# Cross attention in a decoder kernel: query scale and maximum moved into the exponential, its row sums accumulated there, the mask product cut to the x keys

## The reference, cut to what matters

```python
q = rms_norm((x @ wq).reshape(B, L, 16, 128), q_norm_w)
k = rms_norm((x @ wk).reshape(B, L, 4, 128), k_norm_w)
k_ctx = rms_norm((h_ctx_kv @ wk_ctx).reshape(B, T, 4, 128), k_norm_w)
q = q * cos + rotate_half(q) * sin
k = k * cos + rotate_half(k) * sin
k_full = concatenate([k_ctx, k], axis=1)   # 64 context keys, 64 x keys
v_full = concatenate([v_ctx, v], axis=1)
mask = concatenate([zeros((L, T)), causal], axis=1)
scores = einsum('blhd,bmhd->bhlm', q, k_full) / sqrt(128) + mask
probs = softmax(scores, axis=-1)
out = einsum('bhlm,bmhd->blhd', probs, v_full).reshape(B, L, 2048) @ wo
```

## Time and profile before

| | |
|---|---|
| median of 3 runs | 2205.65 us (2205.2 to 2206.36) |
| time of the profiled execution | 2202.77 us |
| its span | 2200.9 us |
| PE busy | 1804.3 us, 82% |
| DVE busy | 1608.8 us, 73% |
| ACT busy | 1061.2 us, 48% |
| POOL busy | 789.9 us, 36% |
| mean granted clock of TensorE | 0.947 |

### The profile page before, as it was taken

How to read it: one execution, slowest core, us unless ns; L and a number is a source line. 1 busy time by engine, 2 the same in 40 slices (tenths; PEclk the granted TensorE clock), 3 DMA queues, 4 the chain that set the end, 5 groups by cost and what they waited for, 6 DMA issues and landing times. The chain is left out here.

```text
span 2200.9 us, 42393 instructions
## 1 busy us (share of the span) xinstructions
PE 1804.3 (82%) x14872; PEld 1064.3 (48%) x14944; DVE 1608.8 (73%) x2887; ACT 1061.2 (48%) x2086; POOL 789.9 (36%) x924
## 2 busy tenths in 40 slices
PE   5999999778889899868874773777777199999998
PEld 2666666446666666654443441222222155555555
DVE  6555555489989989956995996999996447575744
ACT  2444444345555555533332771888888033333322
POOL 5754321366666665547773333112211000000000
PEclk9999999889999999989987995999999599999999
DMA  8511000100000000001110111122221000000000
GB/s 229 140 40 35 21 2 0 44 20 8 11 12 11 7 7 6 1 20 58 57 40 21 42 37 27 44 57 55 59 56 35 24 1 1 10 0 10 0 10 10
DMA packets 71351, 69.74 MB, mean 32 GB/s; under 512 B 14224, under 2 KB 60048, under 8 KB 71184
## 3 DMA queue, kind: packets, MB, share of 16 engines
q1 hardware_dynamic: 70416, 65.46, 10.5%
q0 software_dynamic: 768, 2.10, 0.3%
HBM read 54.16 MB, written 9.96 MB: 29 GB/s over the span
## 5 line engine op out<-in xcount | busy, mean ns | idle before, releaser
L205 PE MATMUL ps<-arena 128*128 128x512 f16 (+6 forms) x6424 | 1106.4, 326 | 76.5 <-POOL arena L1025 20.7
L205 PEld LDWEIGHTS ps<-arena 128*128 128x128 f16 (+1 forms) x6464 | 608.4, 100 | 476.9 <-issue 76.1
L1430 DVE TENSOR_REDUCE arena<-ps 128x4 f32<-128x1024 f32 x256 | 304.7, 1218 | 21.9 <-PE ps L1343 21.9
L1413 ACT ACTIVATE arena<-ps 128x512 f32<-128x512 f32 x512 | 278.5, 598 | 83.8 <-PE ps L1351 60.8
L2121 DVE TENSOR_TENSOR arena<-ps,arena 128x512 f32<-128x512 f32 x96 | 66.4, 691 | 174.4 <-ACT arena L1984 142.2
L1343 PE MATMUL ps<-arena 31*128 31x256 f16 x1024 | 103.3, 278 | 90.2 <-ACT arena L1413 53.6
L1979 ACT ACTIVATE arena<-arena 128x512 f16<-128x512 f32 x96 | 60.4, 629 | 230.3 <-DVE arena L2131 230.2
L1398 PE MATMUL ps<-arena 128*32 128x256 f32 x2048 | 164.0, 392 | 2.6 <-ACT arena L1420 0.6
L534 POOL TENSOR_TENSOR arena<-arena 64x256 f32<-64x256 f32 x128 | 77.9, 609 | 206.8 <-DVE arena L473 195.9
L925 POOL TENSOR_TENSOR arena<-arena 128x512 f32<-128x512 f32 x80 | 107.7, 1346 | 97.6 <-DVE arena L851 97.2
L930 POOL TENSOR_TENSOR arena<-arena 128x512 f32<-128x512 f32 x96 | 105.8, 1102 | 94.0 <-DVE arena L847 87.7
(11 more groups left out here) (205 smaller groups left out, 3114.3 us busy)
## 6 DMA issues: line engine op xcount, KB each, us to landing
arena<-in_L_ffn_gate_up_proj SPq DMA_DIRECT2D x12, 512.0 KB, 3.6
ch_out<-arena SPq DMA_DIRECT2D x32, 128.0 KB
arena<-in_L_ffn_down_proj SPq DMA_DIRECT2D x6, 512.0 KB, 3.6
ch_keys<-arena SPq DMA_DIRECT2D x48, 64.0 KB, 2.0
arena<-ch_keys SPq DMA_DIRECT2D x64, 48.0 KB
arena<-arena SPq DMA_DIRECT2D x192, 16.0 KB
arena<-in_x SPq DMA_DIRECT2D x4, 512.0 KB
arena<-in_L_attn_wq_codes SPq DMA_DIRECT2D x8, 256.0 KB
```

The lines of the kernel that those rows point to most:

```text
L205: last = nc.tensor.matmul(out, a, b, start=start and n == 0, stop=stop and n == len(pairs) - 1, skip_group_check=not group)
L1413: nc.scalar.activation(pT[:, b % 3, g], ps[:, T[n % len(T)], :].rearrange("p (u t) -> p u t", u=KD), ACT.Exp, scale=CH_SCALE).then_inc(s_e ...
L1430: nc.vector.tensor_reduce(m[:, half % 2, 2 * half_pair:2 * half_pair + 2, j, :], ps[:, bank(user):bank(user) + 2, :].rearrange("p g (u s) ...
```

## The change

The queries are rotated and turned without their norm. The norm's factor of each token and head, times 1/sqrt(128), is laid out in a small tile `qscale` by four POOL instructions for each 128 tokens. VectorE still takes the maximum of the raw scores, then multiplies it by `qscale` and -1 into `negtop` (128 x 4) and no longer subtracts. ScalarE computes the exponential straight from PSUM, in four instructions of 128 x 128 in place of one of 128 x 512, each with `qscale` as its scale, `negtop` as its bias and a column of `total` as its accumulator output. The row-sum instruction of VectorE goes. POOL multiplies only the two key turns of a tile by the norm; the flips of the queries wait for the sum (`joined`) in place of the product (`scaled`). The mask product covers the 64 x keys of each of the four blocks, 256 columns in place of 512. The next scores wait for the exponential (`exped`) and no longer for the subtraction (`shifted`), as both read bank SC.

```diff
-                        pe.wait_ge(shifted.sem, shifted.at(i, k))
-                        nc.tensor.matmul(ps[:, SC, :], ident[:, :], mask[:, :, :].rearrange("p a b -> p (a b)"), start=True, stop=False, skip_group_check=True)
+                        pe.wait_ge(exped.sem, exped.at(i, k))
+                        nc.tensor.matmul(ps[:, SC, :].rearrange("p (c m) -> p c m", c=4)[:, :, S:CROSS_KEYS], ident[:, :], mask[:, :, :], start=True, stop=False, skip_group_check=True)
...
-                            pe.wait_ge(scaled.sem, scaled.at(i, n + 1))
+                            if u < 2:
+                                pe.wait_ge(scaled.sem, scaled.at(i, 2 * s + u + 1))
+                            else:
+                                pe.wait_ge(joined.sem, joined.at(i, n + 1))
...
-                        act.wait_ge(shifted.sem, shifted.at(i, k + 1))
+                        act.wait_ge(negated.sem, negated.at(i, k + 1))
                         act.wait_ge(probs.sem, probs.at(i, k - 1))
-                        nc.scalar.activation(e[:, k % 2], shift[:, k % 2], ACT.Exp, scale=CROSS_SCALE).then_inc(exped.sem, 1)
+                        for c in range(4):
+                            last = nc.scalar.activation(e[:, k % 2, c, :], ps[:, SC, c * CROSS_KEYS:(c + 1) * CROSS_KEYS], ACT.Exp,
+                                                        bias=negtop[:, k % 2, c:c + 1], scale=qscale[:, s % 2, g].rearrange("p b r -> p (b r)")[:, c:c + 1],
+                                                        accum_out=total[:, k % 2, c:c + 1])
+                        last.then_inc(exped.sem, 1)
...
-                        dve.wait_ge(probs.sem, probs.at(i, k - 1))
-                        nc.vector.tensor_tensor(shift[:, k % 2], sc, spread(top[:, k % 2, :], CROSS_KEYS), ALU.subtract).then_inc(shifted.sem, 1)
+                        dve.wait_ge(scales_set.sem, scales_set.at(i, 4 * (s + 1)))
+                        nc.vector.scalar_tensor_tensor(out=negtop[:, k % 2, :], in0=top[:, k % 2, :], scalar=-1.0, in1=qscale[:, s % 2, g].rearrange("p b r -> p (b r)"),
+                                                       op0=ALU.mult, op1=ALU.mult).then_inc(negated.sem, 1)
...
-                        nc.vector.tensor_reduce(total[:, k % 2, :], e[:, k % 2], AX.X, ALU.add).then_inc(totalled.sem, 1)
-                        dve.wait_ge(totalled.sem, totalled.at(i, k + 1))
                         nc.vector.reciprocal(inv[:, k % 2, :], total[:, k % 2, :]).then_inc(inverse.sem, 1)
...
-                            a4 = a.rearrange("p (r d) -> p r d", d=CROSS_HD)
-                            nc.gpsimd.tensor_tensor(a4, a4, spread(rms[:, s % 2, u * CROSS_KVH:(u + 1) * CROSS_KVH], CROSS_HD), ALU.mult).then_inc(scaled.sem, 1)
+                            if u < 2:
+                                a4 = a.rearrange("p (r d) -> p r d", d=CROSS_HD)
+                                nc.gpsimd.tensor_tensor(a4, a4, spread(rms[:, s % 2, u * CROSS_KVH:(u + 1) * CROSS_KVH], CROSS_HD), ALU.mult).then_inc(scaled.sem, 1)
+                        if g == 0:
+
+                            pool.wait_ge(exped.sem, exped.at(i, CROSS_KVH * (s - 1)))
+                            heads = rms[:, s % 2, 2 * CROSS_KVH:CROSS_NORMS].rearrange("p (g r h) -> p g r h", r=2, h=2)
+                            pool.wait_ge(scaled.sem, scaled.at(i, 2 * (s + 1)))
+                            for b in range(2):
+                                for r in range(2):
+                                    nc.gpsimd.tensor_scalar(qscale[r * S:(r + 1) * S, s % 2, :, b, :], heads[b * S:(b + 1) * S, :, :, r], CROSS_SCALE, None,
+                                                            ALU.mult).then_inc(scales_set.sem, 1)
+                                    pool.wait_ge(scales_set.sem, scales_set.at(i, 4 * s + 2 * b + r + 1))
```

More of the change, by code:

```diff
@@ L598, in cross_stage @@
     joined = tally("joined", SUBS * CROSS_TURNS)
-    scaled = tally("scaled", SUBS * CROSS_TURNS)
+    scaled = tally("scaled", SUBS * 2)
+    scales_set = tally("scales_set", SUBS * 4)
     turned, turn_kept = tally("turned", SUBS * CROSS_TURNS), tally("turn_kept", SUBS * CROSS_TURNS)
     scored = tally("scored", CROSS_UNITS)
-    maxed, shifted, totalled, inverse = (tally(c, CROSS_UNITS) for c in ("maxed", "shifted", "totalled", "inverse"))
+    maxed, negated, inverse = (tally(c, CROSS_UNITS) for c in ("maxed", "negated", "inverse"))
     exped = tally("exped", CROSS_UNITS)
@@ L629, in cross_stage @@
         qT = sb("qT", [P, 2, 2, CROSS_REP * S], F32)
-        top, total, inv = (sb(c, [P, 2, 4], F32) for c in ("top", "total", "inv"))
-        shift, prob = (sb(c, [P, 2, 4, CROSS_KEYS], F32) for c in ("shift", "prob"))
-        e = shift
+        top, negtop, total, inv = (sb(c, [P, 2, 4], F32) for c in ("top", "negtop", "total", "inv"))
+        qscale = sb("qscale", [P, 2, CROSS_KVH, 2, 2], F32)
+        e, prob = (sb(c, [P, 2, 4, CROSS_KEYS], F32) for c in ("e", "prob"))
         pT = sb("pT", [P, 2, 2, CROSS_REP * S], F32)
@@ L636, in cross_stage @@
         table = sb("table", [P, 2, 2, CROSS_HD], F32)
-        mask = sb("mask", [P, 4, CROSS_KEYS], BF16)
-        maskf = sb("maskf", [P, CROSS_KEYS], F32)
+        mask = sb("mask", [P, 4, S], BF16)
+        maskf = sb("maskf", [P, S], F32)
         ident = sb("ident", [P, P], BF16)
@@ L813, in _ @@
             settle(core, dve, "x")
-            credit(dve, xn, x_lo, summed, rooted, roped, maxed, shifted, totalled, inverse, o_lo, added)
+            credit(dve, xn, x_lo, summed, rooted, roped, maxed, negated, inverse, o_lo, added)
             half = CROSS_HD // 2
@@ L824, in make_tables @@
                 nc.vector.tensor_copy(ident[:, :], core.ident[:, :])
-                nc.vector.tensor_copy(mask[:, :, :], maskf[:, :].unsqueeze(1).broadcast_to([P, 4, CROSS_KEYS]))
+                nc.vector.tensor_copy(mask[:, :, :], maskf[:, :].unsqueeze(1).broadcast_to([P, 4, S]))
                 dve.drain().then_inc(s_tables, 1)
@@ L877, in body @@
                             dve.wait_ge(summed.sem, summed.at(i, CROSS_TURNS * (s + 1)))
-                            dve.wait_ge(scaled.sem, scaled.at(i, CROSS_TURNS * (s - 1)))
+                            dve.wait_ge(scaled.sem, scaled.at(i, 2 * (s - 1)))
+                            dve.wait_ge(scales_set.sem, scales_set.at(i, 4 * (s - 1)))
                             rsqrt(core, dve, rooted, i, RSQRT_STEPS * s, sums[:, s % 2, :], CROSS_RMS_EPS, rms[:, s % 2, :], root)
@@ L904, in _ @@
         def _(pool):
-            credit(pool, c_hi, c_lo, joined, scaled, probs)
+            credit(pool, c_hi, c_lo, joined, scaled, scales_set, probs)
             ctx = core.ins["ctxT"].rearrange("(k p) n -> p k n", p=P)
@@ L2181, in constants @@
     future = key[None, :] > query[:, None]
-    mask = np.concatenate([np.zeros((P, S)), np.where(future, -1e9, 0.0)], 1)
+    mask = np.where(future, -1e30, 0.0)
     start = 2.0 ** (-2.0 ** (-(np.log2(ALIBI_HEADS) - 3)))
```

1 line of the change is left out of this document (added).

## The result

| | before | after |
|---|---|---|
| median of 4 runs | 2206.01 us (2205.20 to 2207.89) | 2232.02 us (2231.38 to 2233.71) |
| profiled execution, its span | 2202.77, 2200.9 us | 2233.71, 2231.9 us |
| mean granted clock | 0.947 | 0.937 |
| the stage, first normalisation row (line 170) of it to that of the next stage | 423.45 to 981.74, 558.3 us | 422.74 to 1004.41, 581.7 us |

The changed kernel is slower: ratio 1.0118 (95% interval 1.0100 to 1.0135), 26 us, where 5 were forecast. The predicted range ended at 2226. In the profiles the stage itself is 23.4 us longer; what follows it took 1219.2 us before and 1227.5 after. In this study's other kernels, whose code there is the same, it took 1217 to 1228, so these 8 us are no more than it varies by without a change there.

A forecast was written before the change was run, and what follows sets the result against it. The prediction took the chain from VectorE's maximum through ScalarE to PE's second flip as the bound. Waits +14.2, mask -5.9 and start -3.2 gave +5.1 us: 2207.9 us profiled, 2211 us median, range 2189 to 2226.

The forecast's parts named there:

- The bound: In the steady stage, one chain from VectorE's maximum through ScalarE to PE's second flip, 36.3 us of waits.
- VectorE's relief: VectorE loses 1.1 us a step, so its lateness at the maximum, 18.2 us in all, is gone.
- The exponentials: On ScalarE, four of 0.36 + 0.20 us each: 2.24 us until the next copy, in place of 0.54.
- Rival 1: Row sums on ScalarE free or nearly so: four exponentials take 1.44 us, total 2188 us; chance 0.32.
- rival 2: Exponentials don't overlap, each accumulator being written out first: 2.72 us, total 2225 us; chance 0.16.
- The product: VectorE's new four-column instruction behind the maximum, priced like the reciprocal: 0.18 us and 0.04 to its reader.
- D: Change in length of the chain from maximum to second flip: forecast +1.20 us; the total changes sign at 1.02.
- 29 D - 29.7: The forecast's total change in us as a function of the chain's lengthening; +5.1 us as forecast.
- The start: Before 495 us, fewer POOL query products give VectorE about 3.1 us, shortening two second-flip waits: -3.2 us.
- The mask: Half of PE's 0.22 us mask product saved over 54 steps, counted in full: -5.9 us.
- The sum: Longer second-flip waits, shorter mask and start together: 14.2 - 5.9 - 3.2 = +5.1 us.
- The sign: Whole kernel slower, by 0.24%; chances slower 0.48, same 0.22, faster 0.30.

The follow-up runs named there:

- i1: The changed kernel with POOL's sum, in steps with a rotation, waiting until VectorE's product is done: 2199.5 us, 0.9965 of the kernel before.
- e4: The kernel before with only the mask product cut to 256 columns: 2205.3 us, 0.9991 of the kernel before.
- e6: The kernel before with its exponential in four instructions, pointer scale and bias, and an accumulator output nothing reads: 2278.6 us, 1.0329 of the kernel before.

## Why the prediction was wrong, step by step

- **The bound** was right: one chain from the maximum through ScalarE to the second flip. So was *VectorE's relief*: it is no longer late, and idles 43.7 us in the window for PE's scores before the maximum.
- **The exponentials** were priced too high, 1.76 us in place of 2.24. Their reader starts 0.44 us behind each, below the 0.515 at which the forecast was to turn faster. Rival 1 (free sums) was not it either, since the accumulator's 0.09 us are there; nor was rival 2.
- **The product** is the first step that failed: "a product over four columns comes, for which the reciprocal's row stands, 0.18 us". It took 0.69 in the steps that count. The text saw the rotation grow beside POOL and used that for the rotation alone, not for the new instruction with two inputs right behind it. Where POOL keeps off, maximum to exponential is 0.92 us (i1) against the forecast's 0.93. With 0.92 and 1.76 the forecast's own sum has D = 0.71, -9 us and 2197; i1 measured 2199.5. With the product's 0.52 us more, D = 1.23 gives +6, 2212: no more than was forecast. The product priced too low and the exponentials priced too high cancel in the sum.
- **The clock** is the second, and the one that the number missed by. The sum, 29 D - 29.7, charges a longer wait with its own length and has no term for the matmuls behind it; no reason is given. Four steps keep PE busy 29.64 us after and 29.14 before, although the mask saves 0.44, and over the stage it is 485.6 against 478.5, although the mask saves 7 (windows view of the stage, before and after, columns as in the earlier trace rows):

```profile
423.45:981.74 558.29, 478.52 (x3008) 343.07 (x3040) 488.13 (x964) 298.45 (x560) 335.08 (x328) 0.95 0.04 13
422.74:1004.41 581.67, 485.61 (x3040) 342.64 (x3040) 413.38 (x900) 378.75 (x1008) 287.51 (x328) 0.92 0.04 12
```

  Before, 32 of the 64 mask products have no record, which leaves up to 1.7 us of PE's work out of the 478.5. So the lower clock cost some 12 us.
- **The start** gave -3.2 us in the forecast. The three second flips ahead of 495 us wait 1.32, 6.50 and 4.25 us after, 12.1, against 1.28, 5.59 and 3.13 before, 10.0: +2.1. From the scores to the maximum it is 4.68 us for 5.32 (463.59 to 468.27, 464.58 to 469.90), 0.6 less and not 3.1, and the product (0.79) and the exponentials took more than that back.
- **The mask**, -5.9 us "in full", is within 0.2% by itself (e4).
- **The sum.** In the stage the forecast had +5.1 us and the profiles show +23.4, 18.3 more. The waits at the second flip grew by 20.3 us (48.8 to 69.1), where the forecast, start included, had 11.0: 9 of the 18, and 5 of these 9 at the start. The clock is some 12. The mask and PE's other idle time take some 3 back. The median's further 2.6 us lie outside the stage and have no cause that was looked for.
- **The sign** was right by luck, with a chance of 0.48. The forecast had it from exponentials of 2.24 us; at their true 1.76 its own sum says 9 us faster, and i1, where the hold-up is gone, is 6 us faster. The kernel is slower for a hold-up and a clock that the forecast didn't have. The range failed since its upper end held a dearer exponential and no dearer clock.

## What to carry to other kernels

Before a small VectorE instruction goes into a chain, look at which of its inputs lie in SBUF and what POOL does in that moment: with two there it waited, at 128 x 4, for the end of POOL's instruction over 512 columns. Where PE waits at one place again and again, ask for two prices of a longer wait, the standing and the matmuls behind it at the lower clock. The second comes in a jump and not in proportion: nothing for 0.28 us more here, and two thirds of the whole for 0.5. Then look for what can leave the chain (here the maximum, or one wait on POOL), not for what makes an engine on it less busy.

## What was not expected of the hardware

A product of 128 x 4 took 161 to 1415 ns, by where POOL's instruction ended. An accumulator output on ScalarE is an instruction with a row of its own, 0.19 to 0.21 us long, that overlaps so far that it costs 0.09. An output product took 2.75 us behind a wait of 1.77 us and 4.44 behind one of 2.32, at a granted clock of 1.00 and 0.62; of the 14 behind waits of 1.9 us or more, 9 were slow. And 1.38 us more of chain, in e6, cost 2.3 us for each of the 32 second flips.
